# State-space layer: the statistics of both normalisations move from VectorE to ScalarE

## The reference

```python
def _layernorm(x, axis=-1, eps=1e-05):
    m = jnp.mean(x, axis=axis, keepdims=True)
    v = jnp.var(x, axis=axis, keepdims=True)
    return (x - m) / jnp.sqrt(v + eps)
...
x = _layernorm(x + _L0_ffn_ref(x, ...), axis=-1)      # norm 1: its result enters the layer
x = _layernorm(x + _L1_attn_ref(x, ...), axis=-1)     # norm 2: behind the layer
...
# in _L1_attn_ref: 256 channels, 16 states
xz = x @ in_proj_w.T
xi, z = jnp.split(xz, 2, axis=-1)
xc = silu(causal convolution of xi, 4 taps)
xp = xc @ x_proj_w.T                                  # gives dt_raw, B, C
dt = jax.nn.softplus(dt_raw @ dt_proj_w.T + dt_proj_b)
dA = jnp.exp(jnp.einsum('bld,dn->bldn', dt, A))
dBx = (dt * x)[..., None] * B[:, :, None, :]
h[t] = dA[t] * h[t-1] + dBx[t];  y[t] = sum over n of h[t, :, n] * C[t, n]
return ((y + xc * D) * jax.nn.silu(z)) @ out_proj_w.T
```

## Time and profile before

| | us |
|---|---|
| median of three runs | 1745.33 |
| the profiled execution | 1742.75 |
| its span, first to last instruction | 1741.0 |
| PE busy | 1393.9 (80%) |
| DVE busy | 1352.9 (78%) |
| POOL busy | 1367.5 (79%) |
| ACT busy | 972.2 (56%) |

### The profile page before, as it was taken

How to read it: one execution, slowest core, us unless ns; L and a number is a source line. 1 busy time by engine, 2 the same in 40 slices (tenths; PEclk the granted TensorE clock), 3 DMA queues, 4 the chain that set the end, 5 groups by cost and what they waited for, 6 DMA issues and landing times.

```text
span 1741.0 us, 23137 instructions
## 1 busy us (share of the span) xinstructions
PE 1393.9 (80%) x5849; PEld 832.6 (48%) x5890; DVE 1352.9 (78%) x2623; ACT 972.2 (56%) x1681; POOL 1367.5 (79%) x949
## 2 busy tenths in 40 slices
PE   5778744426998899889988998898897797999990
PEld 3666643312443344334433443343343476998970
DVE  3888831112999999999999999999999858657777
ACT  2665511104655665566556646655664465887873
POOL 2656566753999999999989989999999477777575
PEclk8999955557999999999989999999899999999995
DMA  5433243325382422342234123312521323555544
GB/s 149 127 101 121 84 89 59 43 40 187 117 254 115 141 84 73 123 140 73 80 127 140 62 86 132 133 56 90 178 80 55 118 69 97 165 155 155 147 107 135
DMA packets 195131, 195.44 MB, mean 112 GB/s; under 512 B 22520, under 2 KB 174008, under 8 KB 190776
## 3 DMA queue, kind: packets, MB, share of 16 engines
q1 hardware_dynamic: 172280, 168.95, 30.0%
q0 software_dynamic: 22784, 25.71, 7.3%
HBM read 137.26 MB, written 59.80 MB: 113 GB/s over the span
## 4 chain that ended last, share of the span: by engine, by line
PE 42%; DVE 26%; issue 15%; POOL 9%; ACT 2%; DMA 2%; DVEq 1%; SPq 1%; POOLq 0%; another core or an unknown queue 0%; ACTq 0%
PE bank L1340 13%; DVE hst L1757 12%; PE bank L1295 6%; PE bank L1433 2%; DVE prod L1779 2%; PE bank L1446 2%; POOL dbx L825 2%; PE bank L1430 2%; PE bank L1457 2%; PE bank L1456 2%; POOL yg L892 2%; PE bank L1329 1%; PE bank L1353 1%; PE bank L1293 1%; POOL xe L759 1%
## 5 line engine op out<-in xcount | busy, mean ns | idle before, releaser
L825 POOL TENSOR_TENSOR dbx<-u,ball 128x1024 f32<-128x1024 f32 x256 | 613.8, 2497 | 5.3 <-POOL u L862 2.8
L1757 DVE TENSOR_TENSOR_SCAN hst<-bank,dbx 128x512 f32<-128x512 f32 x512 | 592.0, 1205 | 11.2 <-POOL dbx L825 6.7
L1340 PE MATMUL bank<-prod,ident 128*128 128x512 f32 x1024 | 514.0, 639 | 23.4 <-DVE prod L1779 18.0
L1029 ACT ACTIVATE bank<-dt,aneg 128x511 f32<-128x511 f32 x512 | 346.4, 688 | 278.8 <-DVE hst L1757 276.8
L1340 PEld LDWEIGHTS bank<-prod,ident 128*128 128x128 f32 x1024 | 207.4, 205 | 263.6 <-issue 209.9
L1779 DVE TENSOR_TENSOR prod<-hst,bank 128x1024 f32<-128x1024 f32 x192 | 233.4, 1216 | 17.2 <-DVE hst L1757 13.8
L834 POOL TENSOR_TENSOR prod<-hst,call 128x1024 f32<-128x1024 f32 x64 | 161.0, 2515 | 22.9 <-DVE hst L1757 22.8
L892 POOL DMA_INDIRECT yg<-expert_rows,row_of x128 | 124.5, 972 | 50.7 <-issue 38.5
L1324 PE MATMUL bank<-parts,sel_c 128*128 128x512 bf16 x152 | 61.1, 403 | 73.8 <-DVE prod L1779 73.1
L1295 PE MATMUL bank<-x2T,inc 128*128 128x512 f32 x256 | 116.5, 598 | 0.0
L880 POOL DMA_INDIRECT sorted_rows<-x3b,row_of x80 | 79.3, 991 | 27.9 <-issue 25.3
(11 more groups left out here) (294 smaller groups left out, 2765.4 us busy)
## 6 DMA issues: line engine op xcount, KB each, us to landing
ball<-b_rows SPq DMA_DIRECT2D x32, 2048.0 KB, 7.1
call<-b_rows SPq DMA_DIRECT2D x16, 1024.0 KB, 9.5
xr<-sorted_rows SPq DMA_DIRECT2D x44, 256.0 KB
expert_rows<-yu SPq DMA_DIRECT2D x44, 256.0 KB, 2.7
sorted_rows<-blank SPq DMA_DIRECT2D x2, 4096.0 KB
xg_rows<-xg SPq DMA_DIRECT2D x16, 320.0 KB, 2.5
xt<-in_x SPq DMA_DIRECT2D x16, 256.0 KB, 2.9
xT<-in_xT SPq DMA_DIRECT2D x16, 256.0 KB, 3.1
```

Source lines behind the costliest of these rows:

```text
L825: gp.tensor_tensor(dbx[n % NDB][:, :, :], u[s.par][:, :, :], ball[:, n:n + 1, :].to_broadcast([P, NH, SEQ]), ALU.mult).then_inc(dbx_rdy, 1)
L1029: act.activation(da_ps[h][:, 1:SEQ], dt_[s.par][:, h, 1:SEQ], ACT.Exp, scale=aneg[:, h, n:n + 1]).then_inc(da_rdy, 1)
L1340: last = mm(y_ps[:, h, :], ident[:, :], from_[:, h, :], start=False, stop=(n == NS - 1), skip_group_check=True)
L1757: dve.tensor_tensor_scan(h_of[:, h, :], da_ps[h][:, :], dbx[n % NDB][:, h, :], 0.0, ALU.mult, ALU.add).then_inc(scan_rdy, 1)
```

## The change

`scale_shift` becomes `scale_of` and keeps two of its four POOL instructions (epsilon and power). The means are no longer taken by DVE. ACT makes them in two passes: `sums` runs each 128 x 128 tile through Identity with a scale of -1/(128 sqrt 128) and a running sum, which leaves minus the mean over sqrt 128 in `shift`; `squares` runs it again through Square with that shift as bias, whose running sum is the variance. The elements themselves are written to a spare buffer, or to `x3o` before it gets its value. DVE gets one small instruction for each norm, `shift_of`, which multiplies `shift` by sqrt 128 and the scale.

```diff
-            def scale_shift(r, n, m, s, ready, done, last):
...
+            def scale_of(r, var, s, ready, done, last):
                 gp.wait_ge(ready, s.at(8, 8))
...
+                gp.tensor_scalar(r[:, :], var[:, :], LN_EPS, None, ALU.add).then_inc(done, 1)
+                gp.wait_ge(done, s.at(3, 1))
                 gp.tensor_tensor(r[:, :], r[:, :], neghalf[:, 0:TT], ALU.pow).then_inc(done, 1)
-                gp.wait_ge(done, s.at(4, 2))
-                settle(gp)
-                gp.tensor_tensor(n[:, :], m[:, :, 0], r[:, :], ALU.mult).then_inc(done, 1)
-                gp.wait_ge(done, s.at(4, 3))
-                settle(gp)
-                gp.tensor_scalar(n[:, :], n[:, :], -1.0, None, ALU.mult).then_inc(done, 1)
...
-                    if m and n == 4:
-                        scale_shift(rs2, nm2, mv2, m, m_mv, m_rs, x3_rdy)
+                    if m and n == 5:
+                        scale_of(rs2, var2, m, m_mv, m_rs, x3_rdy)
...
+            def sums(src, spill, shift, tiles, done):
+                for k in tiles:
+                    act.activation(spill[:, k, :], src[:, k, :], ACT.Identity, scale=-1.0 / (D * ROOT_D), accum_out=shift[:, k:k + 1]
+                                   ).then_inc(done, 1)
+
+            def squares(src, spill, shift, var, s, done):
+                act.wait_ge(done, s.at(8, 4))
+                for k in range(TT):
+                    act.activation(spill[:, k, :], src[:, k, :], ACT.Square, bias=shift[:, k:k + 1], scale=1.0 / ROOT_D,
+                                   accum_out=var[:, k:k + 1]).then_inc(done, 1)
...
-                    if m and n == 5:
-                        act.wait_ge(m_rs, m.at(4, 4))
+                    if m and n == 2:
+                        act.wait_ge(op_mm, m.at(1, 1))
...
+                        sums(blk4(pc_ps), x3o[m.par], shift2, range(TT), m_mv)
+                    if m and n == 4:
+                        squares(blk4(pc_ps), x3o[m.par], shift2, var2, m, m_mv)
+                    if ahead and n == 12:
...
+                        sums(rin[ahead.par], spill, shift1, range(0, 2), f_mv)
+                    if ahead and n == 13:
+                        sums(rin[ahead.par], spill, shift1, range(2, TT), f_mv)
+                    if ahead and n == 14:
+                        squares(rin[ahead.par], spill, shift1, var1, ahead, f_mv)
+                    if m and n == 6:
+                        act.wait_ge(m_rs, m.at(3, 3))
...
+            act.wait_ge(ld_s[0], 16)
+            sums(rin[0], spill, shift1, range(TT), f_mv)
+            squares(rin[0], spill, shift1, var1, Seq(0, 0), f_mv)
             schedule(act, iteration)
...
-            def stats_ahead(s):
...
+            def shift_of(n, shift, r, s, done):
+                dve.wait_ge(done, s.at(3, 2))
+                stt(n[:, :], shift[:, :], ROOT_D, r[:, :], ALU.mult, ALU.mult).then_inc(done, 1)
...
-                    if m and n == 3:
-                        dve.wait_ge(op_mm, m.at(1, 1))
-                        need(dve, m_rs, m.at(4))
-                        stats_of(blk4(pc_ps), st2, mv2, m, m_mv)
+                    if m and n == 6:
+                        shift_of(nm2, shift2, rs2, m, m_rs)
+                    if f and n == 0:
+                        shift_of(nm1, shift1, rs1, f, f_rs)
...
-                    if ahead and n == NS - 2:
-                        stats_ahead(ahead)
...
-            stats_ahead(Seq(0, 0))
```

More of the change, by code:

```diff
@@ L41 @@
 LN_EPS = 1e-5
+ROOT_D = 128 ** 0.5
 BATCH = (6, 6, 4)
@@ L315, in build @@
             x3o = [mb(f"x3o{p}", [P, TT, D]) for p in range(2)]
-            st1 = mb("st1", [P, TT, 6])
-            mv1 = mb("mv1", [P, TT, 2])
+            spill = mb("spill", [P, TT, D])
+            shift1 = mb("shift1", [P, TT])
+            var1 = mb("var1", [P, TT])
             rs1 = mb("rs1", [P, TT])
             nm1 = mb("nm1", [P, TT])
-            st2 = mb("st2", [P, TT, 6])
-            mv2 = mb("mv2", [P, TT, 2])
+            shift2 = mb("shift2", [P, TT])
+            var2 = mb("var2", [P, TT])
             rs2 = mb("rs2", [P, TT])
@@ L808, in scale_shift @@
                 settle(gp)
-                gp.tensor_scalar(r[:, :], m[:, :, 1], LN_EPS, None, ALU.add).then_inc(done, 1)
-                gp.wait_ge(done, s.at(4, 1))
+                gp.tensor_scalar(r[:, :], var[:, :], LN_EPS, None, ALU.add).then_inc(done, 1)
+                gp.wait_ge(done, s.at(3, 1))
                 gp.tensor_tensor(r[:, :], r[:, :], neghalf[:, 0:TT], ALU.pow).then_inc(done, 1)
-                gp.wait_ge(done, s.at(4, 2))
-                settle(gp)
-                gp.tensor_tensor(n[:, :], m[:, :, 0], r[:, :], ALU.mult).then_inc(done, 1)
-                gp.wait_ge(done, s.at(4, 3))
-                settle(gp)
-                gp.tensor_scalar(n[:, :], n[:, :], -1.0, None, ALU.mult).then_inc(done, 1)
             def spread_u(s, n):
@@ L865, in iteration @@
                     if ahead and n == NS - 1:
-                        scale_shift(rs1, nm1, mv1, ahead, f_mv, f_rs, x2_rdy)
+                        scale_of(rs1, var1, ahead, f_mv, f_rs, x2_rdy)
             gp.wait_ge(added, E0 // 2 * 16)
@@ L870, in _ @@
             load_second(Seq(0, 0))
-            scale_shift(rs1, nm1, mv1, Seq(0, 0), f_mv, f_rs, x2_rdy)
+            scale_of(rs1, var1, Seq(0, 0), f_mv, f_rs, x2_rdy)
             schedule(gp, iteration)
@@ L978, in front @@
                 if n == 0:
-                    act.wait_ge(f_rs, s.at(4, 4))
+                    act.wait_ge(f_rs, s.at(3, 3))
                     need(act, res_mm, s.at(1, -1))
@@ L1049, in iteration @@
                         rows_up(0)
-                    if m and n == 5:
-                        act.wait_ge(m_rs, m.at(4, 4))
+                    if m and n == 2:
+                        act.wait_ge(op_mm, m.at(1, 1))
+                        need(act, m_rs, m.at(3))
+                        need(act, st_x3[m.par], m.half(16))
+                        sums(blk4(pc_ps), x3o[m.par], shift2, range(TT), m_mv)
+                    if m and n == 4:
+                        squares(blk4(pc_ps), x3o[m.par], shift2, var2, m, m_mv)
+                    if ahead and n == 12:
+                        act.wait_ge(ld_s[ahead.par], ahead.half(16, 16))
+                        need(act, f_rs, ahead.at(3))
+                        sums(rin[ahead.par], spill, shift1, range(0, 2), f_mv)
[5 more added lines that the diff above has]
+                        act.wait_ge(m_rs, m.at(3, 3))
                         need(act, st_x3[m.par], m.half(16))
@@ L1667, in _ @@
                     group(Seq(j, i))
-            def stats_ahead(s):
-                dve.wait_ge(ld_s[s.par], s.half(16, 16))
-                need(dve, f_rs, s.at(4))
-                stats_of(rin[s.par], st1, mv1, s, f_mv)
+            def shift_of(n, shift, r, s, done):
+                dve.wait_ge(done, s.at(3, 2))
+                stt(n[:, :], shift[:, :], ROOT_D, r[:, :], ALU.mult, ALU.mult).then_inc(done, 1)
             over_h = lambda b: b[:, :].rearrange("p (h t) -> p h t", h=1).to_broadcast([P, NH, SEQ])
```

## The result

The changed kernel takes 1730.7 us (median of 4 runs, 1728.71 to 1734.21) against 1745.99 of the kernel before (4 runs): 15.3 us less, a ratio of 0.9912 with a 95% interval of 0.9892 to 0.9932. The forecast was 1721.6, a gain of 24. The direction and the range hold; a third of the gain is missing. The profiled execution took 1730.68 us, 12.07 less than the one of before.

What follows compares the result with a forecast made beforehand. Each pass was taken as one half set by PE and one by DVE. Early passes 5.1, late passes 19.2, a pass at either side 2.0, prologue -2.6: 23.7 off 1745.33 gives 1721.6 us, range 1709 to 1750.

Steps and rivals of the forecast that it cites:

- The path: PE sets each pass from y to xc, DVE from xc to the next y; only norm 1's 1.32 us counts.
- a sign against it: A pass under 57.0 us would show that norm 2's statistics at n = 3 had a cost, which was denied.
- x3o leaving n = 5: On ACT, x3o's 1.50 us no longer stands ahead of the decays of step 7; no gain counted.
- The clock: PE's slow tail before y mostly goes as its idle becomes 1.83 us; 0.3 us a pass allowed (0 to 1.38).
- Rival B: PE's clock stays low at the tail, so late passes keep their extra 1.38 us; 1728 us, chance 0.11.
- ACT's sets: Four sets of four added ACT instructions a pass, 2.1 us each (1.5 to 2.97), counted as costing 0.
- rival C: ACT's added work delays the decays in DVE's half by 1.6 us a pass; no change, 1742 to 1749, chance 0.08.
- The prologue's chain: For sequence 0 nothing hides the statistics: the way from them to x2 grows by 2.6 us (1.7 to 4.3).
- DVE's addition: `shift_of`, 128 x 4, takes 0.19 us on DVE at n = 0 and at n = 6, hidden by slack.
- Rival A: `shift_of` waits for POOL's running product, 1.2 us on average; 0.5 a pass lost, 1729 us, chance 0.25.
- a cover of its own: Slack to hide a wait of `shift_of`: 0.59 us before prod at n = 0, 1.7 before xc at n = 6.
- a pass at either side: One pass before and one after the 13 counted intervals gain 1.0 us each, 2.0 together.

## Why the prediction was right, and where it was off

The path was right: PE sets one half, DVE the other, and norm 1's 1.32 us count while norm 2's do not. The two runs that move one norm each show it (57.1 us a pass with norm 1 alone, no gain with norm 2 alone). Without the shift's waits passes are 56.94 to 56.98, just under the 57.0 that the prediction had named as a sign against it. The statistics of n = 3 are not the cause. The term is x3o leaving n = 5, for which "nothing is counted": by the rows it is worth the 0.16 us that the scans waited behind it.

The clock was right in kind and too careful in size. I allowed 0.3 us a pass for a tail that is still slow sometimes; the profile after shows 1.00 there, so this term was nothing. Rival B falls. What besides the idle decides the clock stays open, as the early passes of before show.

ACT's sets are shorter than taken (1.1 to 1.6 us against 2.1), and between 600 and 1300 us no scan waits for a decay; rival C falls. The prologue's chain cost 0.9, not 2.6, which is below the lower bound of 1.7 too.

The step that failed is "DVE's addition". I took 0.19 us for `shift_of` from the nearest row of the operation and gave A a chance of 0.25. It takes 0.65 at n = 0 and 2.08 at n = 6 in most passes, and passes are 57.83 instead of 57.33. Rival A's time, 1729, is within 2 us of the result, but that is luck: its split was wrong. I took a wait of 1.2 on average, as for an arrival at random. The arrival is locked to POOL's rhythm: at n = 6 it comes 0.3 us behind the start of a product and pays nearly all of it. And I gave each place a cover of its own, 0.59 and 1.7 us. The slack ahead of xc is one account, from which both draw, and it is nearer 1.6 than 1.7: 0.65 + 2.08 = 2.73 leaves some 1.1 us uncovered. That is what the first half of the pass is longer than in the run with one input from PSUM; the second half is 0.2 shorter, so 57.83 - 56.97 = 0.86 was lost. The run with norm 2's shift mended shows that 0.65 alone is free.

The sum had one more term without a source: 1.0 us for "a pass at either side" of the 13. In the kernel before the last statistics of norm 1 begin at 1246.73 us, so the passes from 1258.05 on have none to lose. In sum, on the spans of the profiled executions (12.0 us): up to the first sum of y 1.7 were lost (the 0.9 of the prologue's chain among them), the next pass gained 0.6, the 13 passes 15.2 instead of 24.3, the pass behind them lost 0.5, the last one with a scan 2.2, and the rest gained 0.6. That last one takes 55.40 us from its L1353 to the y behind it, instead of 53.18; DVE waits there 3.03 for ACT's decay (1.11 before), behind a PE that runs slowly after an idle. The cause of that idle was not tried.

## What to carry to other kernels

Before a small instruction is put on VectorE, look where its inputs lie and what GpSimd runs at that moment. Here, with two tensor inputs in SBUF, an instruction of 128 x 4 paid at least the rest of GpSimd's product, up to 2.3 us, and 7.7 in the place where it got no turn behind it. With one input from PSUM it took 0.15, and as four instructions with a scalar operand 0.55. Waits that are hidden by the same slack must be added up before they are compared with it. And read an instruction's mean against its shape, since such a wait is booked as busy time.

## What the runs showed of the hardware

- A two-input instruction of VectorE got its turn between two back-to-back GpSimd products (2.31 us at most in the changed kernel), but not in a run of products that followed a transfer issued by GpSimd, where the records overlap by some 0.55 us: 7.6 to 9.2 us in 13 passes. That the overlap is the reason is not shown.
- A VectorE instruction with one tensor input and a scalar operand, both in SBUF, does not wait for a running GpSimd product: four in 0.55 us.
- ScalarE reads a running sum by a separate instruction of 0.19 to 0.22 us, which lies under its own tile and the next: four tiles with sums from PSUM took 1.12 us, less than the 1.50 of four without sums, also from PSUM, whose scale and bias are read from SBUF.
- PE's granted clock in the last additions of a late pass was 0.50 behind an idle of 3.15 us in the kernel before, and 1.00 behind idles of 1.03 and 1.55 in the changed one. The idle alone does not decide: behind the same 3.15 us in an early pass (598.06) the eight additions took 5.44 us, not 6.30.
